# Making the first group's memory keys inside the sum of the routed experts

## The reference, cut to what matters

```python
# end of layer 0: x + routed experts, normalised
output_flat = jnp.zeros_like(x_flat).at[sorted_token_idx].add(ff_out)
x = _layernorm(x + output_flat)

# layer 1: B, T, D = 4, 1024, 256; 16 heads of 16; chunks of 64 tokens
q, k, v = proj(Wq), proj(Wk), proj(Wv)            # proj(W) = x @ W.T by head
k = k / jnp.maximum(jnp.linalg.norm(k, axis=-1, keepdims=True), 1e-12)
alpha = jax.nn.sigmoid(alpha_raw) * 0.5
beta = jax.nn.sigmoid(beta_raw) * 2.0
def t_step(M, kv):                                # token by token
    k_t, v_t = kv
    Mk = jnp.einsum('bhde,bhe->bhd', M, k_t)
    return M - alpha * (Mk[..., :, None] * k_t[..., None, :]) + beta * (v_t[..., :, None] * k_t[..., None, :])
```

## Time and profile before

| | |
|---|---|
| three timed runs | 3855.83 us median, 3852.18 to 3858.96 |
| the profiled execution | 3856.25 us, its span 3854.4 us |
| `add_routed` in the trace | 2175.4 to 2231.4 us |
| `memory_projections` in the trace | 2231.4 to about 2481 us |
| mean granted TensorE clock | 0.946 of full |

### The profile page before, as it was taken

The page is one execution under the profiler, slowest core; times in us unless marked ns, Lnnn a source line. Parts: engine busy times, 40 slices in busy tenths (PEclk is TensorE's granted clock), DMA queues, the critical chain, the costliest instruction groups (busy, mean ns, idle before and its releaser), DMA issues. The chain is left out here.

```text
span 3854.4 us, 55275 instructions
## 1 busy us (share of the span) xinstructions
PE 3464.5 (90%) x19490; PEld 1674.9 (43%) x19490; DVE 2232.2 (58%) x3789; ACT 1530.0 (40%) x2333; POOL 1545.5 (40%) x1398
## 2 busy tenths in 40 slices
PE   8989999999999999999799566687888989999995
PEld 3322222222333443333555355343654655556553
DVE  3679999995666236664722548976877521111112
ACT  2257777775444324443123347112652211111112
POOL 3232222224887407887256322143642322222221
PEclk9989999999999999999789776898999999999998
DMA  7833222221112351121522412454541123333333
GB/s 206 222 112 76 64 65 74 76 58 48 44 44 62 104 196 39 47 68 50 172 69 85 153 60 56 172 124 118 173 154 50 34 84 102 93 108 92 103 89 98
DMA packets 314137, 370.57 MB, mean 96 GB/s; under 512 B 56434, under 2 KB 244868, under 8 KB 312900
## 3 DMA queue, kind: packets, MB, share of 16 engines
q1 hardware_dynamic: 268436, 304.79, 25.2%
q0 software_dynamic: 34592, 54.08, 6.8%
q10 hardware_dynamic: 10896, 8.92, 0.8%
HBM read 227.76 MB, written 127.27 MB: 92 GB/s over the span
## 5 line engine op out<-in xcount | busy, mean ns | idle before, releaser
L718 DVE TENSOR_REDUCE heads_mx<-modulated_ring 128x1 f32<-128x512 f32 x976 | 627.8, 683 | 34.2 <-PE modulated_ring L635 28.0
L708 ACT ACTIVATE modulated_probs<-modulated_scores 128x1024 f32<-128x1024 f32 x512 | 496.0, 1021 | 141.3 <-PE modulated_scores L656 141.2
L3487 DVE TENSOR_TENSOR expert_h<-expert_gelu,expert_bank 128x512 f32<-128x512 f32 x128 | 87.9, 687 | 391.2 <-PE expert_bank L3416 391.2
L3458 ACT ACTIVATE expert_gelu<-expert_bank 128x512 f32<-128x512 f32 x128 | 76.4, 597 | 549.3 <-PE expert_bank L3416 549.3
L3376 POOL DMA_INDIRECT scratch_acc<-expert_y,expert_idx x64 | 101.0, 1578 | 433.1 <-DVE expert_y L3492 408.8
L1180 POOL TENSOR_TENSOR causal_total<-causal_total,causal_probs 128x1024 f32<-128x1024 f32 x96 | 227.2, 2366 | 58.9 <-ACT causal_probs L1087 51.5
L1180 POOL TENSOR_TENSOR meta_total<-meta_total,meta_probs 128x1024 f32<-128x1024 f32 x96 | 227.2, 2366 | 58.5 <-ACT meta_probs L1087 51.1
L1109 DVE TENSOR_REDUCE meta_mx<-meta_maxima 128x2 f32<-128x1024 f32 x120 | 146.8, 1224 | 117.6 <-PE meta_maxima L974 117.1
L1109 DVE TENSOR_REDUCE causal_mx<-causal_maxima 128x2 f32<-128x1024 f32 x120 | 146.8, 1224 | 116.8 <-PE causal_maxima L974 116.2
L1087 ACT ACTIVATE causal_probs<-causal_scores 128x1024 f32<-128x1024 f32 x128 | 131.1, 1024 | 142.3 <-PE causal_scores L1000 139.2
L1087 ACT ACTIVATE meta_probs<-meta_scores 128x1024 f32<-128x1024 f32 x128 | 131.0, 1024 | 142.2 <-PE meta_scores L1000 139.2
(11 more groups left out here) (570 smaller groups left out, 7385.0 us busy)
## 6 DMA issues: line engine op xcount, KB each, us to landing
scratch_v<-proj_v SPq DMA_DIRECT2D x8, 1024.0 KB, 6.6
ahead_ctx<-scratch_ctx SPq DMA_DIRECT2D x16, 512.0 KB, 5.6
scratch_M<-steps_snap SPq DMA_DIRECT2D x16, 512.0 KB, 3.3
chunk_raw_v<-scratch_v SPq DMA_DIRECT2D x64, 128.0 KB, 2.8
chunk_mem<-scratch_M SPq DMA_DIRECT2D x32, 256.0 KB, 3.0
first_wg<-x_WgT SPq DMA_DIRECT2D x8, 1024.0 KB, 4.9
first_wu<-x_WuT SPq DMA_DIRECT2D x8, 1024.0 KB, 7.0
first_wd<-x_WdT SPq DMA_DIRECT2D x8, 1024.0 KB, 6.4
```

The lines of the kernel that those rows point to most:

```text
L708: nc.scalar.activation(probs[u % NPROBS][i][:], sc[i][:], ACT.Exp, scale=SCALE).then_inc(s_exp, 1)
L718: V.tensor_reduce(mx[h % 2][:, x // 2, 1 - j % 2, j // 2, x % 2:x % 2 + 1], ring[bank_of["max", 4 * m + j]][:], AX.X, ALU.max).then_inc(s_ ...
```

## The change

- Weights of the memory, gates, identity, `share_of`, the keys of group 0 (`k0`) and the buffer of their transposes (`A1`) are now held over both stages (`hold`, "memory weights"). SP issues the two small gate loads ahead of the first chunk and the three weight loads behind the fourth.
- In `add_routed`, DVE makes scale and shift of chunk k-1 behind the first products of chunk k; ACT copies a chunk's transposes right behind its `new`. The transposes use two banks in place of four; four banks take keys and two their transposes.
- Behind the fourth chunk the keys of group 0 are made inside `add_routed`: projections, squares, lengths, keys and transposes stand between the work of chunks 4 to 7, in an order of their own on each engine.
- `memory_projections` starts with the 16 products of group 0, two sets of four banks in turn; ACT copies out one bank of each tile and DVE three (before two and two). Then come the keys of group 1, all four quarters, then the products of group 1 as before. DVE starts the substitution behind the keys of group 1. Two blanks and the beta row of POOL move behind its last piece of group 0.

```diff
--- before
+++ after
+def turned_of_first_group(scr):
+
+    return scr["memory"]["A1"][:].rearrange("p s h j -> p (s h j)").rearrange("p (m t) -> p m t", m=HH)
...
+def memory_weights(io, scr):
+
+    to = scr["memory"]
+    return [(to["wk"][:], rows(io["m_WkT"])), (to["wv"][:], rows(io["m_WvT"])), (to["wq"][:], rows(io["m_WqT"]))]
+
+
+def memory_gates(io, scr):
+
+    return [(scr["carried"]["gates"][:], column(io["m_alpha16"])), (scr["memory"]["beta"][:], io["m_beta"].partition_broadcast(P))]
...
-        bank = [[st.ps(f"bank{j}{m}", [P, CH]) for m in range(KD)] for j in range(2)]
+        bank = [st.ps(f"bank{m}", [P, CH]) for m in range(KD)]
+        key_bank = [[st.ps(f"key_bank{j}{u}", [P, CH]) for u in range(2)] for j in range(2)]
+        turned_bank = [st.ps(f"turned_bank{m}", [P, CH]) for m in range(HH)]
...
+            load_all(sp, memory_gates(io, scr), s_gates)
             for k in range(BUFFERS):
                 load(k)
+            load_all(sp, memory_weights(io, scr), s_ahead)
...
+            def turn(k):
+
                 act_s.wait(pe, ("new", k))
                 for m in range(KD):
-                    if k >= 2:
-                        act_s.wait(pe, ("turn", k - 2, m))
+                    if k >= 1:
+                        act_s.wait(pe, ("turn", k - 1, m))
                     for t in range(TT):
-                        last = nc.tensor.transpose(bank[k % 2][m][:, t * P:(t + 1) * P], new[k % 2][:, t, m * P:(m + 1) * P], ident[:])
+                        last = nc.tensor.transpose(bank[m][:, t * P:(t + 1) * P], new[k % 2][:, t, m * P:(m + 1) * P], ident[:])
                     mm.done(last, ("turn", k, m))
+
+            def project_keys(c):
+
+                if c >= 2:
+                    keys_dve.wait(pe, ("k", c - 2, 1))
+                for t in range(TT):
+                    for kd in range(KD):
+                        last = nc.tensor.matmul(key_bank[c % 2][t // 2][:, (t % 2) * D:(t % 2 + 1) * D], every_16th(scr["xT"][0][:, kd, :])[:, c * TT + t, :], wk[:, kd, :],
+                                                start=(kd == 0), stop=(kd == KD - 1))
+                keys_mm.done(last, ("k", c))
+
+            def turn_keys(c):
+
+                keys_dve.wait(pe, ("k", c, 1))
+                for m in range(HH):
+                    if c >= 1:
+                        keys_act.wait(pe, ("kT", c - 1, m))
+                    for t in range(TT):
+                        last = nc.tensor.transpose(turned_bank[m][:, t * P:(t + 1) * P], k0[:, c * TT + t, m * P:(m + 1) * P], ident[:])
+                    keys_mm.done(last, ("kT", c, m))
+
+            pe.wait_ge(s_made, 2)
+            for k in range(QUADS):
+                turn(k)
+            pe.wait_ge(s_ahead, ahead)
+            act_s.wait(pe, ("turn", QUADS - 1, KD - 1))
+            project_keys(0)
+            turn(4)
+            project_keys(1)
+            turn(5)
+            turn_keys(0)
+            project_keys(2)
+            turn(6)
+            turn_keys(1)
+            project_keys(3)
+            turn(7)
+            turn_keys(2)
+            turn_keys(3)
...
-            root(0)
-            for k in CHUNKS:
-                if k + 1 < NCH:
-                    root(k + 1)
...
+            act.wait_ge(s_gates, gates)
+            nc.scalar.activation(raw[:], raw[:], ACT.Sigmoid).then_inc(s_share, 1)
+            nc.scalar.activation(beta[:], beta[:], ACT.Sigmoid).then_inc(s_share, 1)
+            root(0)
+            for k in range(QUADS):
+                normed(k)
+                turned(k)
+                root(k + 1)
+            normed(4)
+            squared(0)
+            turned(4)
+            root(5)
+            root_of_keys(0)
+            normed(5)
+            squared(1)
+            turned(5)
+            root(6)
+            root_of_keys(1)
+            turned_keys(0)
+            normed(6)
+            squared(2)
+            turned(6)
+            root(7)
+            normed(7)
+            turned_keys(1)
+            root_of_keys(2)
+            squared(3)
+            turned(7)
+            turned_keys(2)
+            root_of_keys(3)
+            turned_keys(3)
...
                     dve_s.done(V.scalar_tensor_tensor(part[k % 2][:, t, :], ya[j][:, t, :], share(0, t), kept_rows(scr, k)[:, t // 2, t % 2, :], ALU.mult, ALU.add), ("first", k, t))
+                if k:
+                    factors(k - 1)
                 for t in range(TT):
...
+            def measure_keys(c):
+
+                for u in range(2):
+                    keys_act.wait(dve, ("square", c, u))
+                    keys_dve.done(V.tensor_reduce(length2[c % 2][:, u * 2 * H16:(u + 1) * 2 * H16], square[u][:].rearrange("p x (h d) -> p (x h) d", d=HD16), AX.X, ALU.add),
+                                  ("length", c, u))
+
+            def make_keys(c):
+
+                keys_act.wait(dve, ("sqrt", c))
+                keys_dve.done(V.tensor_scalar(bounded[c % 2][:], length[c % 2][:], 1e-12, None, ALU.max), ("bounded", c))
+                keys_dve.wait(dve, ("bounded", c))
+                keys_dve.done(V.reciprocal(inv[c % 2][:], bounded[c % 2][:]), ("inv", c))
+                keys_dve.wait(dve, ("inv", c))
+                for u in range(2):
+                    x = c * TT + 2 * u
+                    keys_dve.done(V.tensor_tensor(k0[:, x:x + 2, :].rearrange("p x (h d) -> p (x h) d", d=HD16), key_bank[c % 2][u][:].rearrange("p (h d) -> p h d", d=HD16),
+                                                  inv[c % 2][:, u * 2 * H16:(u + 1) * 2 * H16].unsqueeze(2).broadcast_to([P, 2 * H16, HD16]), ALU.mult), ("k", c, u))
...
+            for k in range(QUADS + 2):
+                sum_and_measure(k)
+            measure_keys(0)
+            sum_and_measure(6)
+            make_keys(0)
+            measure_keys(1)
+            sum_and_measure(7)
+            make_keys(1)
+            factors(7)
+            measure_keys(2)
+            make_keys(2)
+            measure_keys(3)
+            make_keys(3)
...
-        A = two("A", [P, SUB, H16, SUB])
-        laid = [A[1][:].rearrange("p s h j -> p (s h j)").rearrange("p (m t) -> p m t", m=HH), st.sb("laid", [P, HH, GROUP])[:]]
+        A = [st.sb("A0", [P, SUB, H16, SUB]), scr["memory"]["A1"]]
+        laid = [turned_of_first_group(scr), st.sb("laid", [P, HH, GROUP])[:]]
...
-        FIRST = [(0, c) for c in range(QUADS)] + [(1, 0)]
-        AMONG = {4 * c - 3: c for c in range(1, QUADS + 1)}
         turned = lambda g, c: [("kT", g, c, m) for m in range(HH)]
-        OTHER_BANKS = {0: (3, 7, 11, 14), 1: range(0, TILES, 2)}
         jobs = []
-        for n in range(len(FIRST) + 1):
-            jobs += ([("k", *FIRST[n])] if n < len(FIRST) else []) + (turned(0, n - 2) if n >= 2 else [])
-        for t in range(TILES):
-            if t in AMONG:
-                jobs += turned(1, AMONG[t] - 1) + [("k", 1, AMONG[t])] * (AMONG[t] < QUADS)
-            jobs += [("dots", 0, t)]
-        for t in range(TILES):
-            jobs += [("dots", 1, t)]
+        jobs += [("dots", 0, t) for t in range(TILES)]
+        for c in range(QUADS + 2):
+            jobs += [("k", 1, c)] * (c < QUADS) + (turned(1, c - 2) if c >= 2 else [])
+        jobs += [("dots", 1, t) for t in range(TILES)]
...
-                return [2 * (n % 3) + u if g == 0 else 4 + u for u in range(2)]
+                return [2 * ((n + 2 * g) % 3) + u for u in range(2)]
...
-                return [4 * (n in OTHER_BANKS[g]) + p for p in range(4)]
+                return [4 * ((n + 1) % 2) + p for p in range(4)]
...
-        ACT_BANKS = {0: (0, 1), 1: (0, 1, 2, 3)}
-        DVE_BANKS = {0: (2, 3), 1: ()}
+        ACT_BANKS = {0: (0,), 1: (0, 1, 2, 3)}
+        DVE_BANKS = {0: (1, 2, 3), 1: ()}
...
-            load_all(sp, weights[0:3], s_w)
-            load_all(sp, weights[3:], s_wide)
             for g in range(G):
                 if g == 0:
-                    act_s.wait(sp, ("kT", 0, QUADS - 1, HH - 1))
                     sp.dma_start(rows(scr["kT"])[:, :, 0:GROUP], laid[0]).then_inc(s_kT, 16)
...
-            fill_identity(nc, pool, ident[:], s_made)
-            fill_blocks(nc, pool, blocks[:], s_made, 2)
-            nc.gpsimd.memset(carried["v"][:], 0.0).then_inc(s_blank, 1)
-            nc.gpsimd.memset(carried["s"][:], 0.0).then_inc(s_blank, 1)
-            pool.wait_ge(s_beta, 1)
-            nc.gpsimd.tensor_scalar(carried["beta_row"][:].rearrange("p (h d) -> p h d", d=HD16), beta[:].unsqueeze(2).broadcast_to([P, H16, HD16]),
-                                    2.0, None, ALU.mult)
-            pool.wait_ge(s_share, 4)
...
+            nc.gpsimd.memset(carried["v"][:], 0.0).then_inc(s_blank, 1)
+            nc.gpsimd.memset(carried["s"][:], 0.0).then_inc(s_blank, 1)
+            nc.gpsimd.tensor_scalar(carried["beta_row"][:].rearrange("p (h d) -> p h d", d=HD16), beta[:].unsqueeze(2).broadcast_to([P, H16, HD16]),
+                                    2.0, None, ALU.mult)
...
```

(22 more changed lines are left out.)

168 lines of the change are left out of this document (79 added, 89 removed).

## The result

| | before | changed |
|---|---|---|
| median | 3854.73 us (3852.18 to 3858.96, 4 runs) | 3826.69 us (3823.95 to 3829.32, 4 runs) |
| ratio to before | 1 | 0.9925 [0.9913, 0.9937] |
| span of the profiled execution | 3854.4 us | 3822.2 us |

The kernel became 28.0 us faster; 25 were forecast, and the 3831 us forecast are 4.3 over the median. The windows of the changed kernel answer to the earlier trace rows (stretch, us, busy PE, PEld, DVE, ACT, POOL, clock, DMA, GB/s): the sum, the products of group 0, the keys of group 1, the substitution.

The account below looks back on a forecast made before the run. DVE's substitution bounds the last stretch, so its start counts. The sum grows 22 us, stage start to substitution falls from 110.6 to 63.6: 25 us earlier, 3831 us from 3856.25 profiled (timed median 0.4 lower); range 3818 to 3847.

Parts of the forecast that it names:

- The yardstick: Start of the substitution, at 2341.95 us before: forecast at 2317.0, 25 us earlier, with all that follows only shifted.
- Ahead of chunk 4: In the sum of the experts: factors 3.3 us earlier, chunk period 0.5 later, gate loads 1.5 later.
- The chain through the lists: From `new` of chunk 3 to the sum's end, through projections, keys and chunks: 46.8 us, bounds 41 and 52.
- projection 3: Last projection of group 0's keys in the sum: 6.6 us at the low clock, behind an idle PE.
- GpSimd's ring: Products of group 0: POOL sees the copy-out, issues, masks; PE multiplies, copies follow: 6.7 to 6.9 us for three tiles, 2.3 each.
- the buffer's ring: Products of group 0: copy-out, third issue, landing 2.4 us, copies 2.1, hand-overs: 6 us for three tiles, 2.0 each.
- Slower: Rival, chance 0.05: buffer ring with slow landings, 4.3 us a tile in group 0's products, 30 us more, 3861 us.
- The keys of group 1: All quarters in one run behind group 0's products, up to the substitution: 25.8 us, bounds 22.8 and 27.5.
- What could take it back: Group 1's products lag 7.9 us more, leaving 3.7 us of cover before its substitution; costed 0.
- the full-clock rival: Rival, chance 0.11: PE stays at the full clock; chain 41 us, 2.1 a tile, keys 22.8; 3819 us.
- the slow one: Rival, chance 0.17: PE low and rings slow; the sum's chain 52 us, 2.9 a tile; 3845 us.
- the gain would not come: Rival, chance 0.04: group 0's keys run between the sum's chunks, not beside them, 46 us; 3855 us.

## Why the prediction was right, point by point

**The yardstick held.** What follows the substitution's start only shifted: 136.3 us to the end of both groups before, 136.4 after. The substitution's start came 28.5 us earlier for 25 forecast.

**Ahead of chunk 4.** Forecast 1.3 us earlier for `new` of chunk 3, measured 2.3. The gate loads cost 1.1 (DVE's first row +6.6 for +5.5) against 1.5, and the period stayed at 5.30, not 5.4 to 5.5: `new` at 2194.59 and 2199.89. ACT has 0.46 to 0.48 us of idle time for DVE's factors ahead of each, and the copies fit beside it.

**The chain through the lists was right in its links and too long in two.** From `new` of chunk 3 to the end of the sum 46.8 were forecast and 43.0 measured. TensorE's rows in the changed sum, against the earlier trace rows:

```profile
2204.77 5.92 PE L1970 MATMUL blend_key_bank<-mproj_wk,x_turned 128*128 128x256 f32 x16 [0.78 <-ACT blend_std L2006]
2210.53 1.04 PE L1961 MATMUL blend_bank<-mproj_ident,blend_new 128*128 128x128 f32 x8
2211.40 3.79 PE L1970 MATMUL blend_key_bank<-mproj_wk,x_turned 128*128 128x256 f32 x16
...
2221.93 4.17 PE L1970 MATMUL blend_key_bank<-mproj_wk,x_turned 128*128 128x256 f32 x16
...
2229.59 3.78 PE L1970 MATMUL blend_key_bank<-mproj_wk,x_turned 128*128 128x256 f32 x16
```

Only the first projection was slow, 5.92 us. The last ran at the full clock (3.78 and not 6.6): together 3.5 of the 3.8 us. The mis-sized term is projection 3, taken at the low clock for its idle time ahead: the transposes in front of it had waited only 1.68 us, not the 3.23 of the earlier trace rows. The rest of the chain measured what it was summed to: from the end of projection 3 to the last copy 9.5 us for 9.8. Its end on ACT, where the earlier trace rows had the last copy of `x_turned`:

```profile
2240.96 1.88 ACT L2043 ACTIVATE mproj_A<-blend_turned_bank 128x512 f32<-128x512 f32 x2 [3.29 <-PE blend_turned_bank L1981]
```

**The products: the wrong ring.** This is the step that failed. 2.3 us a tile were forecast from GpSimd's ring, with 2.0 for the buffer's; measured were 2.57 (2.60 if the 15 periods are counted from copy to copy), and the runs show the buffer's ring as the one that binds. Its terms can be read off tile 0. DVE's last copy of it ends near 2248.6 (the first six of twelve). Then GpSimd's issues, TensorE's tiles 3 and 4, and ACT's next copy into the buffer:

```profile
2249.30 1.13 POOL L2276 DMA_DIRECT2D mproj_A<-mproj_dots  x2 [1.62 <-ACT mproj_dots L2378]
```

```profile
2251.65 4.10 PE L2372 MATMUL mproj_bank<-mproj_A,mproj_masked 32*128 32x128 f32 x64 [0.61 <-POOL mproj_masked L2329]
```

```profile
2254.25 0.38 ACT L2378 ACTIVATE mproj_dots<-mproj_bank 128x256 f32<-128x256 f32 x1 [2.10 <-DMA mproj_A<-mproj_dots]
```

From copied out to the next copy into the same buffer are 5.6 us, with 2.1 of copies 7.7 for three tiles, 2.57 each. The sum had 3.9 for those 5.6: 1.2 to the last issue, 2.4 landing and hand-overs. The piece that comes last is not GpSimd's, whose second issue starts at 2249.90. It is SP's third: its issue starts at 2250.67, 2.0 us behind the copy, and it lands 3.5 us later, at 2254.17, just ahead of ACT's copy. So the last issue was mis-sized by 0.8 and the landing by 1.1. GpSimd's ring is hardly shorter: it issues until 2250.43, masks tile 3, and that tile's products end near 2253.7, 0.5 us ahead of the copy that waits for the landing. With the two rings so close, it fits that a fourth buffer gave only 0.25 us a tile.

Tile 0 is one tile. Where the earlier trace rows had 2.4, the median over all of group 0's pieces is now, for GpSimd's:

```profile
mproj_A<-mproj_dots POOLq DMA_DIRECT2D x32, 16.0 KB, 3.0
```

The 2.4 was of a stage with a tile every 4.3 us (68.6 for 16), and of GpSimd's pieces only; SP's had 2.6 there. From the first mask to the last product it made 42.1 us for the 37.5 forecast, 4.6 more. That is the mechanism of the rival *Slower* at a small size: it decides from 4.0 us a tile. TensorE's tile at the low clock was short by a little too, 2.09 us for 1.9.

**The keys of group 1**: 23.1 us for 25.8. They start right behind the last product, with the clock on its way up (12.02 us for three projections; the earlier trace rows has 13.66). The last quarter's keys at 2307.32 are the releaser of the substitution, as forecast.

**Sum**: -1.0 at chunk 3, -3.8 in the chain, -0.6 at the stage's start, +4.6 in the products, -2.7 in the keys, so -3.5 against the forecast +141.6: +138.1. One large error up and two down, of 3 to 5 us each: that the total is within 3.5 us is luck, for it is better than its parts.

**What could take it back**: nothing did. ACT went on behind the second group's products at 2373.22, 3.45 us ahead of its substitution at 2376.67; 3.7 of cover were forecast.

```profile
2373.22 1.09 ACT L2378 ACTIVATE mproj_dots<-mproj_bank 128x512 f32<-128x512 f32 x2 [6.17 <-DMA mproj_A<-mproj_dots]
```

**The rivals.** In the sum the full-clock rival was nearer (projections at 3.78 to 4.17, chain 43 for its 41), and in the keys of group 1 too (23.1 for its 22.8). The products lie half-way to the slow one (2.57 between 2.3 and its 2.9). Each is half right, in opposite signs. That the gain would not come, since keys run between the chunks and not beside them, is refuted by the sum's end at +72.4, where with the keys behind all chunks it is +83.9; and even that kernel kept 19.1 us.

## What to carry to other kernels

When a stage is packed closer, price its transfers from a stretch where they follow one another as closely, and are as many, as they will be, not from the loose stage they come from: the 2.4 us became 3.0 and 4.2. Write each ring over a set of buffers out to its last piece, whoever issues it, since one more buffer is the cheapest test of it. And read stages from a point inside the same trace, and take a second trace of the same code for the spread: here that told about 4 us, where totals told 10.
